# Causal attention: the first 24 fills of scores and their row maxima, made in the stage before

## The reference, cut to what matters

```python
q = (x @ wq.T).reshape(B, S, N_HEADS, HEAD_DIM)        # 16 heads of 8
k = (x @ wk.T).reshape(B, S, N_KV_HEADS, HEAD_DIM)     # 4 heads of 8, each used by 4 query heads
v = (x @ wv.T).reshape(B, S, N_KV_HEADS, HEAD_DIM)
attn = jnp.einsum('bqhd,bkhd->bhqk', q, k) * scale
attn = jnp.where(causal, attn, -jnp.inf)
attn = jax.nn.softmax(attn, axis=-1)
out = jnp.einsum('bhqk,bkhd->bqhd', attn, v).reshape(B, S, C)
```

## Time and profile before

| what | us |
|---|---|
| median of 3 runs (693.75 to 694.32) | 693.75 |
| the profiled execution, its own time | 693.14 |
| its span, from first to last instruction | 691.4 |
| PE busy | 553.2 (80%) |
| VectorE busy | 506.6 (73%) |
| ScalarE busy | 360.6 (52%) |
| GpSimd busy | 267.8 (39%) |

### The profile page before, as it was taken

The page is one execution under the profiler, slowest core; times in us unless marked ns, Lnnn a source line. Parts: engine busy times, 40 slices in busy tenths (PEclk is TensorE's granted clock), DMA queues, the critical chain, the costliest instruction groups (busy, mean ns, idle before and its releaser), DMA issues. The chain is left out here.

```text
span 691.4 us, 11852 instructions
## 1 busy us (share of the span) xinstructions
PE 553.2 (80%) x3810; PEld 310.3 (45%) x3810; DVE 506.6 (73%) x2314; ACT 360.6 (52%) x738; POOL 267.8 (39%) x499
## 2 busy tenths in 40 slices
PE   1866478738868899577999999999998898898870
PEld 1856367737657556311233333333333464455420
DVE  5699999361382777488989999999997155369784
ACT  5841034500120467501478878888788745466762
POOL 2001007620002276700244544545455444265874
PEclk9997665555986799955599999999999998899996
DMA  8000000000000056410011211111110000000001
GB/s 311 2 1 1 0 1 1 0 1 0 1 1 1 0 174 199 165 35 4 3 36 33 62 30 35 34 33 49 45 36 1 7 1 1 2 0 16 32 16 61
DMA packets 17580, 24.77 MB, mean 36 GB/s; under 512 B 3246, under 2 KB 14014, under 8 KB 17342
## 3 DMA queue, kind: packets, MB, share of 16 engines
q1 hardware_dynamic: 16942, 21.91, 10.2%
q10 hardware_dynamic: 576, 2.10, 0.8%
HBM read 13.65 MB, written 10.35 MB: 35 GB/s over the span
## 5 line engine op out<-in xcount | busy, mean ns | idle before, releaser
L1422 DVE CUSTOM_DVE_ANT_0 d_masked_S<-d_pS,d_wide_mask 128x512 bf16<-128x512 f32 (+3 forms) x512 | 217.0, 485 | 15.2 <-PE d_pS L1546 10.3
L1520 ACT ACTIVATE d_P<-d_pT 128x768 f32<-128x768 f32 (+1 forms) x192 | 165.9, 882 | 62.2 <-PE d_pT L1546 60.6
L1390 POOL TENSOR_SCALAR_AFFINE_SELECT d_P<-d_P 128x256 f32<-128x256 f32 x256 | 102.6, 415 | 133.8 <-ACT d_P L1520 133.7
L1546 PE MATMUL d_pS<-Ks,Qs 48*128 48x512 bf16 (+3 forms) x512 | 109.9, 332 | 19.7 <-DVE d_mx L1422 9.0
L1546 PE MATMUL d_pO<-d_P,V 128*32 128x512 f32 (+3 forms) x1024 | 98.5, 460 | 1.4 <-POOL d_P L1390 0.9
L1546 PE MATMUL d_pT<-Qs,Ks 51*128 51x512 bf16 (+3 forms) x512 | 72.5, 311 | 2.0 <-ACT d_mT L1490 2.0
L1546 PEld LDWEIGHTS d_pS<-Ks,Qs 48*128 48x128 bf16 x512 | 34.8, 96 | 72.2 <-DVE d_mx L1422 62.2
L1546 PEld LDWEIGHTS d_pT<-Qs,Ks 51*128 51x128 bf16 x512 | 20.7, 94 | 74.0 <-ACT d_P L1520 42.7
L1889 PE MATMUL e_PE<-gate_expT,w_qkvT 128*128 128x512 f32 x96 | 46.9, 634 | 6.9 <-DVE e_T L1763 4.0
L1763 DVE SCALAR_TENSOR_TENSOR e_T<-e_PE,comb,e_T 128x128 f32<-128x128 f32 x128 | 35.2, 342 | 20.9 <-ACT e_T L1866 20.8
L1866 ACT ACTIVATE e_T<-e_PE,comb 128x128 f32<-128x128 f32 x128 | 35.9, 373 | 25.8 <-issue 14.6
(11 more groups left out here) (308 smaller groups left out, 1015.1 us busy)
## 6 DMA issues: line engine op xcount, KB each, us to landing
Qs<-q_stack SPq DMA_DIRECT2D x32, 192.0 KB, 3.0
q_stack<-Qp SPq DMA_DIRECT2D x8, 384.0 KB, 2.6
X<-in_x_dram ACTq DMA_DIRECT2D x4, 512.0 KB, 6.4
q_stack<-Qp SPq DMA_DIRECT2D x8, 256.0 KB, 2.5
out_dram<-e_moe SPq DMA_DIRECT2D x8, 256.0 KB, 2.0
w_qkvT<-in_w_qkvT_dram SPq DMA_DIRECT2D x1, 1536.0 KB
Ks<-k_stack SPq DMA_DIRECT2D x32, 48.0 KB, 3.2
q_stack<-Qp SPq DMA_DIRECT2D x8, 128.0 KB, 2.1
```

What stands on the lines that cost most here:

```text
L1390: last = nc.gpsimd.affine_select(out=view, in_=view, compare_op=ALU.is_ge, fill=0.0, base=0, pattern=[[0, 2], [1, 128]], channel_multiplie ...
L1422: last = nc.vector.tensor_tensor_reduce(out=out_[:, at:at + w], in0=src[:, at:at + w], in1=wide_mask[:, 512 - w:512], scale=1.0, scalar=LO ...
L1520: nc.scalar.activation(P[pair % 4][:, :, P_AT[unit]:P_AT[unit] + w], pT[(3 * pair + unit) % 2][:, :, 0:w], ACT.Exp, scale=float(HD4) ** -0 ...
L1546: return nc.tensor.matmul(out, lhsT, rhs, start=start, stop=stop)
```

## The change

24 of batch 0's 48 fills, with their maxima, move from the causal stage's opening into the projections' stage, in a ring of two banks, PY[0] and PY[1]. PE makes fills 0 and 1 ahead of `by_channel(7)`, 2 to 4 between it and `project(7)`, and 5 to 23 behind. VectorE takes maxima 0 to 5 ahead of `rests(7)`, 6 and 7 behind it, and 8 to 23 behind `values(7)`. The `keep_busy` matmuls of the last batch are dropped (4 and 6). The mask's set-up moves to the start of VectorE's work in the projections' stage. The maxima, the wide mask and the masked scores get places that outlive the stage, in `hadamard` and `w_qkvT`, which are no longer in use by then. S and S_max become semaphores of the whole program.

```diff
+AHEAD = 24
+FILLS = [(k + j, f) for k in range(0, HEADS, 2) for f in range(3) for j in range(2)]
+SPANS = (((3, 0),), ((2, 0),), ((1, 0), (0, 256)))
+def scores(nc, top, dst, c, k, f):
+    rows = slice(64 * (k % 2), 64 * (k % 2) + SLOTS * HD4)
+    h = ORDER[k]
+    for q, at in SPANS[f]:
+        w = 128 * q + 128
+        last = nc.tensor.matmul(dst[:, at:at + w], top.Qs[c][rows, h % 8, 128 * q:128 * q + 128],
+                                top.Ks[c][rows, h // 4 % 2, 0:w], start=True, stop=True)
+    return last
+def row_maxima(nc, top, src, junk, c, k, f):
+    for q, at in SPANS[f]:
+        w = 128 * q + 128
+        last = nc.vector.tensor_tensor_reduce(
+            out=junk[:, at:at + w], in0=src[:, at:at + w], in1=top.wide_mask[:, 512 - w:512], scale=1.0,
+            scalar=LOWEST, op0=ALU.add, op1=ALU.max, accum_out=top.mx[c][:, q, ORDER[k]:ORDER[k] + 1])
+    return last
...
+        S_ring = [PY[k][:, :, :].rearrange("p r d -> p (r d)") for k in two]
+        LAST = B - 1
...
+                def maxima_ahead(first, end):
+                    for i in range(first, end):
+                        k, f = FILLS[i]
+                        dve.wait_ge(top.scores["S"], i + 1)
+                        row_maxima(nc, top, S_ring[i % 2], top.masked_S[i % 3], 0, k, f)\
+                            .then_inc(top.scores["S_max"], 1)
                 dve.wait_ge(sm["zeroed"], 2)
+                nc.vector.memset(top.wide_mask[:, 0:384], 0.0)
+                nc.vector.tensor_copy(top.wide_mask[:, 384:512], top.mask_bf[:, :]).then_inc(top.scores["mask_wide"], 1)
+                dve.wait_ge(top.scores["mask_wide"], 1)
...
+                    if turn - 1 == LAST:
+                        maxima_ahead(0, 6)
                     if turn - 1 in batches:
                         rests(turn - 1)
+                    if turn - 1 == LAST:
+                        maxima_ahead(6, 8)
+                maxima_ahead(8, AHEAD)
...
+                def scores_ahead(first, end):
+                    for i in range(first, end):
+                        k, f = FILLS[i]
+                        if i == 0:
+                            pe.wait_ge(top.stacks[0][0], 64)
+                        if i < 2:
+                            pe.wait_ge(sm["x"], LAST + i)
+                        else:
+                            pe.wait_ge(top.scores["S_max"], i - 1)
+                        scores(nc, top, S_ring[i % 2], 0, k, f).then_inc(top.scores["S"], 1)
                 for turn in TURNS:
                     if turn + 1 in batches:
                         attended(turn + 1)
-                    if turn - 1 in batches:
+                    if turn - 1 in batches[:LAST]:
                         keep_busy(turn - 1, 4)
                         by_channel(turn - 1)
                         keep_busy(turn - 1, 6)
                         project(turn - 1)
+                scores_ahead(0, 2)
+                by_channel(LAST)
+                scores_ahead(2, 5)
+                project(LAST)
+                scores_ahead(5, AHEAD)
...
-                nc.vector.memset(wide_mask[:, 0:384], 0.0)
-                nc.vector.tensor_copy(wide_mask[:, 384:512], top.mask_bf[:, :]).then_inc(sm["mask_wide"], 1)
-                dve.wait_ge(sm["mask_wide"], 1)
-                maxima(0, 0, everything)
+                maxima(0, 0, FILLS[AHEAD:])
...
-                first(0, 0, 0, everything)
+                first(0, 0, 0, FILLS[AHEAD:])
                 rows(0, 0)
...
+        top.scores = top.sems("mask_wide S S_max")
...
+        top.mx = [top.hadamard[:, 64 * c:64 * c + 64].rearrange("p (q h) -> p q h", q=QT) for c in range(2)]
+        spare = spare[:, 2, :, :].bitcast(BF16).rearrange("p n (a t) -> p (n a) t", t=512)
+        top.wide_mask, top.masked_S = spare[:, 0, :], [spare[:, 1 + k, :] for k in range(3)]
```

More of the change, by code:

```diff
@@ L881, in gated_attention_phase @@
         ph.close()
+AHEAD = 24
+ORDER = [8 * a + i for i in range(HEADS // 2) for a in range(2)]
+FILLS = [(k + j, f) for k in range(0, HEADS, 2) for f in range(3) for j in range(2)]
[15 more added lines that the diff above has]
+    return last
 def load_stack(sp, top, dram, b, u):
@@ L1240, in causal_attention_phase @@
         ph = Phase(nc, ctx, "d_")
-        sm = ph.sems("mask_wide S S_max part1 rest1 part2 rest2 parts mT_psum mT ST P masked PV O_sb O_T O_raw rden O_tok half_power")
+        sm = ph.sems("part1 rest1 part2 rest2 parts mT_psum mT ST P masked PV O_sb O_T O_raw rden O_tok half_power")
         two = range(2)
@@ L1248, in causal_attention_phase @@
         Qs, Ks, stacks = top.Qs, top.Ks, top.stacks
-        mx = [ph.sb(f"mx{c}", [128, QT, HEADS]) for c in two]
+        mx, S_made, S_max = top.mx, top.scores["S"], top.scores["S_max"]
         rest = [ph.sb(f"rest{c}", [128, 2, QT, HEADS]) for c in two]
@@ L1257, in causal_attention_phase @@
         rden = [ph.sb(f"rden{k}", [128, QT, 2, 4]) for k in two]
-        wide_mask = ph.sb("wide_mask", [128, 512], BF16)
-        masked_S = [ph.sb(f"masked_S{k}", [128, 512], BF16) for k in range(RING)]
         ring = ph.ps("pS", [128, RING, 512])
@@ L1269, in causal_attention_phase @@
         half = lambda a, n: slice(64 * a, 64 * a + n)
-        ORDER = [8 * a + i for i in range(HEADS // 2) for a in two]
         P_AT = (0, 512, 896, 1152)
@@ L1322, in early_steps @@
             return [(steps[u - CHUNK_TURNS * k], k) for k in range(EARLY) if u - CHUNK_TURNS * k in steps]
-        everything = [(k + j, f) for k in range(0, HEADS, 2) for f in range(3) for j in two]
         fill_of = lambda k, f: 6 * (k // 2) + 2 * f + k % 2
@@ L1365, in split @@
                 def split(n, c):
-                    pool.wait_ge(sm["S_max"], n * NS + NS)
+                    pool.wait_ge(S_max, n * NS + NS)
                     nc.gpsimd.tensor_copy(m3[c][:, :, 0, :], mx[c][:, :, :]).then_inc(sm["part1"], 1)
@@ L1416, in maxima @@
                     for k, f in some:
[L1417 to L1426, removed]
+                        fill = fill_of(k, f)
+                        dve.wait_ge(S_made, n * NS + fill + 1)
+                        row_maxima(nc, top, pS[fill % RING], top.masked_S[fill % RING], c, k, f).then_inc(S_max, 1)
                 def invert(n, g):
@@ L1471, in early_turn @@
                             weigh(nc, dve, top, k)
-                nc.vector.memset(wide_mask[:, 0:384], 0.0)
-                nc.vector.tensor_copy(wide_mask[:, 384:512], top.mask_bf[:, :]).then_inc(sm["mask_wide"], 1)
-                dve.wait_ge(sm["mask_wide"], 1)
-                maxima(0, 0, everything)
-                maxima(1, 1, everything[:6 * LEAD])
+                maxima(0, 0, FILLS[AHEAD:])
+                maxima(1, 1, FILLS[:6 * LEAD])
                 steps(step)
@@ L1550, in first @@
                     for k, f in some:
-                        h, i, a, fill = ORDER[k], ORDER[k] % 8, k % 2, fill_of(k, f)
+                        fill = fill_of(k, f)
                         if k % 8 == 0 and f == 0:
                             pe.wait_ge(stacks[c][k // 8], 64 * m + 64)
[L1554 to L1560, removed]
+                        wait(pe, S_max, n * NS + fill - RING + 1)
+                        scores(nc, top, pS[fill % RING], c, k, f).then_inc(S_made, 1)
                 def second(n, m, c, pair, unit, more):
@@ L1627, in early_turn @@
                         if step == "attention_by_channel":
-                            pe.wait_ge(sm["S_max"], B * NS)
+                            pe.wait_ge(S_max, B * NS)
                             pe.wait_ge(sm["O_tok"], 2 * (NG // 2) * (k + 1))
@@ L1639, in early_turn @@
                             gate(nc, pe, top, logits, k)
-                first(0, 0, 0, everything)
+                first(0, 0, 0, FILLS[AHEAD:])
                 rows(0, 0)
-                first(1, 0, 1, everything[:6 * LEAD])
+                first(1, 0, 1, FILLS[:6 * LEAD])
                 steps(step)
```

## The result

The changed kernel took 687.74 us (median of 7 runs, 685.5 to 689.67) against 693.75 for the kernel before on the same chip (median of 7): a ratio of 0.992, 95% interval 0.9901 to 0.9939, so 4.2 to 6.9 us faster. The forecast was 690.4 with a range of 687.7 to 692.5. The sign and the mechanism of case A are right. The time lies at the range's lower end, beside case B's 688.1, for another reason than B's: the clock did fall. That it lies in the range at all, by 0.04 us, is luck. A's own range (689.2 to 691.6) missed it, and the profiles show a smaller gain than the timed runs, as the part on why the prediction was right says.

What follows compares the result with a forecast made beforehand. VectorE alone was taken to bound the causal stage's opening. With project(7), ring and set-up counted, 24 fills there end at 319.7 against 323.0: gain 3.3 us off the median 693.75 gives 690.4, range 687.7 to 692.5.

Steps and rivals of the forecast that it cites:

- case A: The forecast itself: TensorE at half clock in project(7), 690.4 us, own range 689.2 to 691.6; chance 0.50.
- case B: Rival: the clock holds until project(7) is done, gain 5.7 us, time 688.1; chance 0.25.
- What bounds the opening: Causal stage's opening: VectorE alone bounds batch 0's 48 maxima, 26.4 us, 13.2 for 24; loss there moves the end one for one.
- The order bites: End of projections: fill 5 is issued behind project(7), so rests(7) waits behind its maximum; VectorE idle about 4 to 5 us.
- The clock: Last batch without its 10 fillers: TensorE's clock likelier than not has fallen to half when project(7) starts.
- The size of project(7): Last batch's projection: 5.2 us taken, against 2.9 before; bounds 2.9 (no fall) and 5.8 (all at half the pace).
- The set-up: Start of projections: the mask's memset and copy delay batch 0; 0.2 us taken, bounds 0 and 0.35.
- The ring of two: Fills 8 to 23 at half clock: VectorE waits on refills with two buffers, sixteen fills take 9.9 us.
- The boundary: From the end of VectorE's maxima ahead to the start of the causal stage: 1.0 us.
- Rival D: No gain: an unseen wait holds VectorE, so the 24 maxima only move the stage's end out; 693.7 us, chance 0.05.
- rival E: Slower: the ring of two runs in series, each fill after the previous maximum; a loss of 8 us, chance 0.07.
- rival C: The clock costs elsewhere: three to four us more at half clock cost 1.5 to 2; 691.9 to 692.5, chance 0.13.

Runs made afterwards that it cites:

- e3: Kernel after the change, with VectorE doing both of the last batch's subtractions ahead of maximum 5: 686.75 us, ratio 0.9915 to the kernel before.
- e8: Kernel after the change, unchanged, run again: 687.67 us, ratio 0.9934 to the kernel before.
- e2: Kernel after the change, with the last batch's filler matmuls put back (4 and 6): 687.77 us, ratio 0.9917 to the kernel before.
- e4: Kernel before the change, with only the last batch's filler matmuls left out, nothing moved ahead: 693.29 us, ratio 0.9992.
- e1: Kernel before the change, unchanged, run again: 693.50 us, ratio 1.0005.
- e5: Kernel after the change, with PQ[0] as a third bank in the ring of fills made ahead: 687.82 us, ratio 0.9925 to the kernel before.

## Why the prediction was right, and where its sizes were off

*What bounds the opening* was right: VectorE fills without a gap, and what is behind slides. From the last maximum to the first exponential it is 12.09 us before and after; the turns behind that are longer after the change (below).

*The order bites* was right: 3.97 us of idle time before maximum 5 (4 to 5 were named), the K subtraction behind it, and e3 gets 1.0 us back by the order alone.

*The clock* was right, and the rival B wrong. It fell 0.3 us ahead of project(7) (in e8 0.2 us behind its start), and e2 and e4 show that the fillers decide it, in the kernel with the moves and in the one without. By the rule of the Trainium skill ("TensorE: Matmul & The Clock Gate", the section on why this matters for kernels) that idle gaps between bursts are what loses it, it would have held. Here it fell though PE's longest gap was 1.1 us, so the trace disagrees with the rule taken alone.

*The size of project(7)* was off, and is the term that was mis-sized: "I take 5.2". It took 4.4, and the clock was at the full level again when V and fill 5 were issued. I let the half clock last, and the windows show that it came back at 290.2, while the projections ran. Counted from batch 6's subtraction, maximum 5 started at 8.8 us and not at 9.6. The forecast's sum, 3.3, holds the set-up's 0.2, which lies outside D, so that its D was to fall by 3.5. D fell by 4.5, and fill 5's 0.8 and the boundary's 0.1 are most of the difference.

*The set-up* was put at 0.2. The first statistics came 0.54 us later behind the stage's start (4.87 to 5.41):

```profile
223.83 0.22 DVE L1065 MEMSET w_qkvT<- 128x192 uint32 x1 [5.98 <-POOL V L995]
224.06 0.20 DVE L1066 COPY w_qkvT<-mask_bf 128x128 bf16<-128x128 bf16 x1
224.29 0.89 DVE L1006 BATCH_NORM_STATS2 c_y_st<-c_PY 128x6 f32<-128x128 f32 x4
```

Compare 222.39 in the earlier trace rows. From the stage's start to batch 6's K subtraction it is 64.06 us in the profile before (64.02 in e1) and 64.06 and 64.28 in the two after, but these don't all open the stage at the same clock. The first two matmuls in the profile after and in e8:

```profile
218.92 0.45 PE L1146 MATMUL c_PY<-Y,selT 32*128 32x128 f32 x2 [1.60 <-PEq L58]
```

```profile
217.51 0.61 PE L1146 MATMUL c_PY<-Y,selT 32*128 32x128 f32 x2 [1.60 <-PEq L58]
```

They took 0.62 and 0.69 us before and in e1, and 0.45 in e4, which has no moved set-up. Like with like it is 64.06 against e4's 63.70, and 64.28 against 64.06 and 64.02. So 0.2 to 0.4 of the set-up is left by then, and "I take 0.2" was about right. Where the rest of the 0.54 goes wasn't tried.

*The ring of two* was right: 9.9 predicted, 9.97 measured, and e5 takes it away. *The boundary* was 0.9 and not 1.0. SyncE's and GpSimd's slide was hidden as expected.

*From 4.5 to the measured 6.0.* The opening is 4.5 us shorter in both pairs of profiles (41.43 and 41.45 against 36.92 and 36.98). The set-up takes 0.2 to 0.4 of it back, and so do the turns in part. From the first exponential to the last maximum of all they last 196.26 and 196.27 us in the two profiles before, 196.47 and 197.14 in the two after. The clock rises later there, 12.9 and 13.1 us behind the first exponential where it was 12.3 in both before. The windows with the rise, before and after (at 347.4 and 344.8):

```profile
347.00:348.00 1.00, 1.00 (x12) 0.18 (x12) 0.26 (x4) 0.17 (x1) 0.39 (x2) 0.79 0.00 0
```

```profile
344.00:345.00 1.00, 1.00 (x8) 0.13 (x4) 0.12 (x2) 0.09 (x1) 0.25 (x1) 0.59 0.00 0
```

All in all it is 313.84 us from the start of the projections' stage to the last maximum in both profiles before, and 309.54 and 310.50 after: a gain of 3.3 to 4.3 us, about the forecast's 3.3. The timed runs say 6.0 by the medians, 5.5 by the ratio (4.2 to 6.9), and on the second chip 4.6 (0.9934, 2.6 to 6.6). Nothing that was found belongs to the change beyond the 3.3 to 4.3, and where the rest of the 6.0 comes from stays open.

Rival D is out by the profile, rival E by the 9.97 us, and rival C was there only in part: the clock rose 0.6 to 0.8 us later in the turns' work, as above, and the turns were 0.2 to 0.9 us longer. Turns that don't slide as one were named as a sign that the prediction is wrong; by this much they didn't. The stages that the change doesn't touch differed by more: the projections' stage began between 213.9 and 219.6 us in the twelve profiles, and the part behind the last maximum lasted 156.4 to 160.2 us. That isn't the change's doing, since it differs as much between two profiles of one kernel (157.4 and 160.2).

## What to carry to other kernels

Work moved into an idle stretch gains the idle time and no more: move as much as fills it up to what ends the stage otherwise, here, by D and F, 16 fills and not 24. In an in-order queue the moved work must not stand ahead of something that others wait for; one index (fill 5 ahead of the subtractions) cost 1.0 us. Filler matmuls that seem useless beside new work may still be what holds the clock, so weigh them against the matmuls that stand behind, and leave a ring as deep as it was.

## What the runs showed of the hardware

In the profile after TensorE's clock fell while PE's gaps were 1.1 us and shorter, ahead of it five fills of 48 rows and four transposes. In all eight profiles without the ten fillers project(7) was slow (4.4 to 4.6 us), in none of the four with them (2.9). It came back during project(7), while PE was busy 1.00 of each us. Its changes aren't tied to the program: two executions of the same code have them at other places. In the two profiles of the kernel after, the projections' first two matmuls took 0.45 and 0.61 us, and the part from the last maximum to the end 157.4 and 160.2 us.

On a span of 690 us single runs of one kernel differ by 3 to 7 us, where D repeats within 0.1. The mean granted clock of a run goes with this: of the 23 timed runs of the kernel before on e8's chip, the two shortest (spans of 686.1 and 686.3 us) had 0.847, the two longest (692.8 both) 0.840, and over all 23 the correlation of span and clock is -0.86 (-0.84 and -0.78 on the two other chips). That the clock makes the whole of the spread isn't shown by this.
